# Causal attention core: six bf16 copies of queries and keys against two float32r parts in two row tiles of TensorE

## What is computed

```
q = rope(q); k = rope(k)                      # 32 query heads, 8 key/value heads, head size 16
scores = einsum('bqhd,bkhd->bhqk', q, k) / 16 # 4 query heads share a key head
scores = where(causal, scores, -inf)          # 1024 x 1024 per head
ctx = einsum('bhqk,bkhd->bqhd', softmax(scores), v)
out = ctx @ w_dense.T + b_dense
```

## Time and profile before

| | us |
|---|---|
| median of 3 runs | 1276.73 |
| the profiled execution, own time | 1276.3 |
| its span, first to last instruction | 1274.5 |
| projections block (from its first transposes) | 343 to 403.4 |
| prologue of the core (maxima of group 0) | 403.4 to 438.9 |
| groups 0 to 7 | 438.9 to 687.1 |
| output product | 687.1 to about 720 |

### The profile page before, as it was taken

How to read it: one execution, slowest core, us unless ns; L and a number is a source line. 1 busy time by engine, 2 the same in 40 slices (tenths; PEclk the granted TensorE clock), 3 DMA queues, 4 the chain that set the end, 5 groups by cost and what they waited for, 6 DMA issues and landing times. The chain is left out here.

```text
span 1274.5 us, 21579 instructions
## 1 busy us (share of the span) xinstructions
PE 1097.4 (86%) x5654; PEld 717.9 (56%) x5655; DVE 905.9 (71%) x1775; ACT 704.8 (55%) x1218; POOL 566.7 (44%) x582
## 2 busy tenths in 40 slices
PE   4969999999194899999997787999999947878597
PEld 3847777777182233333333675677777735467454
DVE  5869888887575888888860666888888847444632
ACT  3238787887143177777775131787888824424142
POOL 4335666664556244443331225566666545140200
PEclk9979999999596599999998888999999977989889
DMA  9367899764615550000000183789995561000001
GB/s 351 114 220 185 218 243 286 174 114 60 192 50 155 104 99 19 1 1 1 1 1 1 63 309 111 236 196 258 275 222 103 83 156 67 1 1 1 0 1 66
DMA packets 62798, 151.01 MB, mean 118 GB/s; under 512 B 12224, under 2 KB 17024, under 8 KB 58240
## 3 DMA queue, kind: packets, MB, share of 16 engines
q1 hardware_dynamic: 37440, 95.17, 22.3%
q0 software_dynamic: 22592, 50.27, 20.3%
q10 hardware_dynamic: 2688, 4.65, 1.1%
HBM read 104.89 MB, written 44.97 MB: 118 GB/s over the span
## 5 line engine op out<-in xcount | busy, mean ns | idle before, releaser
L811 POOL DMA_INDIRECT moe_acc_rows<-xn,moe_token_of x94 | 208.0, 2213 | 146.3 <-ACT xn L886 131.1
L923 DVE TENSOR_TENSOR moe_w_lo<-moe_raw,moe_w_hi 128x1536 fp32r<-128x1536 f32 x94 | 165.4, 1759 | 62.9 <-ACT moe_w_hi L874 62.7
L1977 ACT ACTIVATE causal_prob<-causal_sc 128x512 f32<-128x512 f32 (+3 forms) x384 | 166.8, 492 | 70.3 <-PE causal_sc L1882 69.7
L874 ACT CAST moe_w_hi<-moe_raw 128x1536 fp32r x94 | 138.7, 1475 | 78.0 <-issue 76.4
L1864 PE MATMUL causal_mx<-ks,causal_qs 96*128 (+4 forms) x384 | 131.4, 353 | 23.0 <-DMA causal_qs<-causal_parts 16.5
L831 PE MATMUL moe_gu<-moe_w_hi,xt_hi 128*128 128x512 f32 x282 | 148.4, 526 | 0.6 <-DVE moe_w_lo L923 0.6
L1882 PE MATMUL causal_sc<-causal_qs,ks 99*128 (+3 forms) x384 | 120.2, 333 | 1.9 <-ACT causal_prob L1977 1.7
L831 PE MATMUL moe_gu<-moe_w_hi,xt_lo 128*128 128x512 f32 x282 | 111.8, 396 | 0.0
L831 PE MATMUL moe_gu<-moe_w_lo,xt_hi 128*128 128x512 f32 x282 | 110.9, 393 | 0.0
L826 PE MATMUL moe_gu<-moe_raw,xn 128*128 x188 | 98.0, 603 | 5.0 <-ACT moe_w_hi L874 5.0
L1808 POOL TENSOR_SCALAR_AFFINE_SELECT causal_prob<-causal_prob 128x512 f32<-128x512 f32 x64 | 40.9, 639 | 115.9 <-ACT causal_prob L1977 115.5
(11 more groups left out here) (317 smaller groups left out, 2724.5 us busy)
## 6 DMA issues: line engine op xcount, KB each, us to landing
moe_raw<-in_w_gu SPq DMA_DIRECT2D x34, 1024.0 KB, 6.1
moe_raw<-in_w_down SPq DMA_DIRECT2D x34, 512.0 KB, 8.2
causal_qs<-causal_parts SPq DMA_DIRECT2D x45, 128.0 KB, 3.6
moe_acc_rows<-moe_zeros SPq DMA_DIRECT2D x2, 2304.0 KB, 14.7
moe_acc_rows<-x SPq DMA_DIRECT2D x18, 256.0 KB, 2.0
moe_xn_rows<-xn SPq DMA_DIRECT2D x2, 2048.0 KB, 10.7
x<-moe_acc_rows SPq DMA_DIRECT2D x16, 256.0 KB, 6.8
xn<-moe_acc_rows ACTq DMA_DIRECT2D x16, 256.0 KB, 7.2
```

What stands on the lines that cost most here:

```text
L811: pool.indirect_dma_start(acc_rows[a], bass.IndirectOffsetOnAxis(ap=token_of[:, b - 3:b - 2].bitcast(U32), axis=0), out_rows[(b - 3) % OUT ...
L874: nc.scalar.copy(w_hi[1 - s][:, :, :], raw[:, bass.ds(at + SPLIT_AT, GU_COLS - SPLIT_AT)].rearrange("p (k n) -> p k n", k=SPLIT)).then_inc ...
L923: nc.vector.tensor_tensor(w_lo[1 - s][:, :, :], raw[:, bass.ds(at + SPLIT_AT, GU_COLS - SPLIT_AT)].rearrange("p (k n) -> p k n", k=SPLIT), ...
L1977: nc.scalar.activation(prob[u % 2][:, h, o:CH], sc[(u * QPK + h) % BANKS][:, o:CH], ACT.Exp, scale=SCALE).then_inc(exp_done, 1)
```

## The change

Queries and keys are now cut into **two** float32r parts instead of three bf16 ones. Three products of parts suffice, so a stack is 48 rows high. POOL's subtraction writes the second part itself; ACT's second cast and DVE's third part are gone. The maximum has two parts and two rows, so the scores contract over 50 rows.

The stack is held twice. Partitions 0 to 49 serve the scores, partitions 64 to 111 the maxima. A matmul of at most 64 rows is issued to a tile of 64 by 128 of the array: the scores to the tile that starts at row 0, the maxima to the one at row 64. The order of PE's matmuls is unchanged. Both buffers now hold two groups (`g % 2`) in float32, are loaded twice (once per tile), and each load waits until the products that read the old content are done. PE's loop over groups is unrolled, since the addresses are constants.

```diff
-    Q_PART = (0, 0, 1, 0, 1, 2)
-    K_PART = (0, 1, 0, 2, 1, 0)
-    STACK = len(Q_PART) * HD
-    MROWS = 3
+    Q_PART = (0, 0, 1)
+    K_PART = (0, 1, 0)
+    MROWS = 2
+    MAX_AT = 2 * HD
+    SCORE_ROWS = slice(0, 3 * HD + MROWS)
+    MAXIMA_ROWS = slice(64, 64 + 3 * HD)
+    IN_SCORES = (0, HD, 2 * HD + MROWS)
+    IN_MAXIMA = (64, 64 + HD, 64 + 2 * HD)
...
-            nc.gpsimd.tensor_tensor(rest[r % 2][:, :], turned[r % 2][:, :], part[r % NPB][:, 0, :],
-                                    ALU.subtract).then_inc(rest_done, 1)
+            nc.gpsimd.tensor_tensor(part[r % NPB][:, 1, :], turned[r % 2][:, :], part[r % NPB][:, 0, :].bitcast(F32),
+                                    ALU.subtract).then_inc(part_lo_done, 1)
...
-            nc.scalar.copy(part[r % NPB][:, 1, :], rest[r % 2][:, :]).then_inc(p2_done, 1)
...
-            nc.vector.tensor_tensor(part[r % NPB][:, 2, :], rest[r % 2][:, :], part[r % NPB][:, 1, :],
-                                    ALU.subtract).then_inc(p3_done, 1)
...
# SP, the core: loads
-                    with sp.Fori(1, KV) as g:
-                        sp.wait_ge(stack_in, g * (16 * LOADS) - 16 * LOADS // 2)
-                        load(g)
+                    load(IN_MAXIMA, 1, for_maxima_in)
+                    for g in range(KV - 1):
+                        if g:
+                            sp.wait_ge(sc_done, g * NS * QPK)
+                        load(IN_SCORES, g + 1, for_scores_in)
...
+                        if g + 2 < KV:
+                            sp.wait_ge(mx_done, (g + 1) * NMU)
+                            load(IN_MAXIMA, g + 2, for_maxima_in)
...
# PE: maxima
-                        nc.tensor.matmul(mx[i % BANKS][:, 0:w], qs[0:STACK, bass.ds(at, P)],
-                                         ks[0:STACK, bass.ds(gn * S + kc * CH, w)], start=True, stop=True).then_inc(mx_done, 1)
+                        nc.tensor.matmul(mx[i % BANKS][:, 0:w], q_r[MAXIMA_ROWS, at:at + P], k_r[MAXIMA_ROWS, key:key + w],
+                                         start=True, stop=True).then_inc(mx_done, 1)
# PE: scores
-                        nc.tensor.matmul(sc[b][:, o:CH], ks[0:STACK + MROWS, bass.ds(g * S + kb * P, P)],
-                                         qs[0:STACK + MROWS, bass.ds(g * QG + (h * S + c * CH + o), CH - o)],
-                                         start=True, stop=True).then_inc(sc_done, 1)
+                        nc.tensor.matmul(sc[b][:, o:CH], k_r[SCORE_ROWS, key:key + P], q_r[SCORE_ROWS, at + o:at + CH],
+                                         start=True, stop=True).then_inc(sc_done, 1)
...
-                    group(0, True, True)
-                    with pe.Fori(1, KV - 1) as g:
-                        group(g, False, True)
-                    group(KV - 1, False, False)
+                    for g in range(KV):
+                        group(g, g == 0, g < KV - 1)
```

More of the change, by code:

```diff
@@ L1420, in sem, with load_keys @@
             return m.semaphore(f"{name}_{what}")
-        parts_dram = nc.dram_tensor(f"{name}_parts", [3, QK_ROWS, S], BF16, kind="Internal").ap()
-        v_all, ks, ident = m.v_all, m.ks, m.ident_half
-        consts, stack_in, ones_done = sem("consts"), sem("stack_in"), sem("ones_done")
+        parts_dram = nc.dram_tensor(f"{name}_parts", [2, QK_ROWS, S], F32, kind="Internal").ap()
+        v_all = m.v_all
+        ks = outer.enter_context(nc.sbuf_tensor(f"{name}_keys", [P, 2 * 2 * S], BF16))[:, :]
+        for_scores_in, for_maxima_in, ones_done = sem("for_scores_in"), sem("for_maxima_in"), sem("ones_done")
+        def load_keys(eng, rows, g, done):
+            at = g % 2 * S
+            for a, row in enumerate(rows):
+                eng.dma_start(ks.bitcast(F32)[row:row + HD, at:at + S],
+                              parts_dram[K_PART[a], g * HD:(g + 1) * HD, :]).then_inc(done, 16)
         dense_in, wd_half, wd_ready, x_biased = sem("dense_in"), sem("wd_half"), sem("wd_ready"), sem("x_biased")
@@ L1445, in causal_attention_layer @@
             turned = [sb(f"turned{s}", [P, CH]) for s in range(2)]
-            rest = [sb(f"rest{s}", [P, CH]) for s in range(2)]
             NPB = 4
-            part = [sb(f"part{s}", [P, 3, CH], BF16) for s in range(NPB)]
+            part = [sb(f"part{s}", [P, 2, CH], F32R) for s in range(NPB)]
             vt = sb("vt", [P, S])
@@ L1582, in _ @@
                     act.wait_ge(c_in, 48)
-                    for n in range(UNITS + 4):
+                    for n in range(UNITS + 2):
                         if n < UNITS:
@@ L1664, in _ @@
                     lo(T - 1)
-                    for n in range(2, UNITS + 4):
+                    for n in range(2, UNITS + 1):
                         if n in number:
@@ L1700, in causal_attention_layer @@
             neg = sb("neg", [P, TC, QPK])
[L1701 to L1703 removed]
+            neg_parts = [sb(f"neg_parts{h}", [P, TC, MROWS, QPK], F32R) for h in range(NCH)]
+            neg_turned = [sb(f"neg_turned{h}", [MROWS * QPK, CH]) for h in range(NCH)]
             prob = [sb(f"prob{s}", [P, QPK, CH]) for s in range(2)]
@@ L1986, in group @@
                                 read_maxima(g + 1, 0)
-                    for a in range(1, len(Q_PART), 2):
-                        first_queries(act, a)
+                    load_queries(act, IN_MAXIMA, 0, 1, for_maxima_in)
+                    for a in range(len(Q_PART)):
+                        load_queries(act, IN_SCORES, 0, a, for_scores_in)
                     nc.scalar.activation(warm[:, :], m.ident[0:1, 0:1], ACT.Exp).then_inc(exp_done, BANKS)
```

100 lines of the change are left out of this document (41 added, 59 removed).

## The result

The changed kernel takes 1353.42 us (median of 4 runs, 1344.75 to 1360.92) against 1276.55 of before (4 runs as well): ratio 1.0603, interval 1.0532 to 1.0674, slower. The prediction said 1261.5 and faster, and was wrong. The profiled execution took 1344.75 us, its span 1343.0. It was the fastest of the four: the profiles differ by 68.5 us, the medians by 76.9. What follows takes the 68.5 apart.

A forecast was written before the change was run, and what follows sets the result against it. Three nearly equal needs per group (PE 28.7 us, DVE 26.3, the exponential-to-score circle 27.9) were taken as bound, tied by PE's fixed order. Terms of 12.6 + 2.0 + 0 + 0.4 = 15.0 us off gave about 1261.5 us, range 1250 to 1270.

The forecast's parts named there:

- SP's loads stand at nothing: Groups: 12 DMAs, 2 MB, issued at a group's start and needed 29 us later, so priced at no cost.
- rival D: Groups: PE's thinner work lets the clock fall to about 0.5; +60 us, near 1340; chance 0.04.
- Rival B: Groups 1 to 6: loads delay POOL's maxima rows before step 4, up to 1.9 us each; 1272.5 us; chance 0.20.
- Term 3: Core's start: PE's wait for the first queries, 6.5 us into the core, taken as unchanged, 0 us.
- Group 7 held 1.00 with PE busy 22.1 of 27.9 us: Group 7, before the change: full clock without maxima, cited against the falling clock of rival D.
- Term 1: Groups: score and maxima matmuls run side by side in two tiles; groups 1 to 6 take 29.6 us, 12.6 us off altogether.
- C (no overlap): Groups: the two tiles do not overlap, so PE stays the largest need; 1289 us, slower; chance 0.11.
- Rival A: Groups: full relief, DVE and the circle run past each other; groups take 27.4 us, 1246 in all; chance 0.10.
- Term 2: End of the projections: the last unit's shorter way to DRAM takes 2.0 us off, bounds 1.0 and 2.6.
- Term 4: Prologue: DVE-bound, 25.0 us of work, nearly unchanged; 0.4 us off, bounds 0 and 0.8.

The follow-up runs named there:

- late_loads: Changed kernel, but SP issues a group's twelve loads only after its second-half maxima rows have landed: 1312.4 us, in three rounds 1309.0 (ratio 1.0238).
- bf16_pair: Kernel before with 48-row bf16 stacks in both tiles, three of six products left out, loads far ahead, PE's loop unrolled: 1282.9 us.
- full7: late_loads with group 7's scores from step 1 over the whole array, and the mask loaded before the first queries: 1303.4 us.
- bf16_pair7: bf16_pair with group 7's scores from step 1 over 112 rows, the whole array: 1278.9 us, ratio 1.0021.
- whole_f32r: Changed kernel's float32r parts without row tiles: scores and maxima over 66 rows on the whole array, one copy, loads late: 1306.5 us.
- unrolled: Kernel before with PE's loop over groups 1 to 6 written out, nothing else: 1276.4 us, in five rounds 1275.4 (ratio 1.000).
- stack4: Kernel before with four bf16 products instead of six, scores over 67 rows (whole array), maxima in a 64-row tile, PE's loop unrolled: 1462.3 us.

## Why the prediction was wrong

**The two steps that failed** are "SP's loads stand at nothing" and the dismissal of rival D.

- *Loads.* The step asked when the loads themselves are needed, not what stands behind them. Rival B named the place, the instructions and the direction, and was priced at 1.9 us a group from the earlier trace rows, where other loads were under way. The runs show waits of up to 7.9: POOL's rows waited until nearly all of the loads in front were through, which took 16 to 17 us and not rival B's 6 to 11. Even with those numbers the issue after 6.5 us (now up to 9) should have been priced as the rest of the queue. 33 us, and 3 more in the prologue, where the mask and the first queries stood among bytes needed later. Term 3 was right on PE's first matmul (6.3 us into the core for 6.5) and missed DVE's wait for the mask:

```profile
409.93 0.70 DVE L2006 CUSTOM_DVE_ANT_0 causal_mx<-causal_mx,causal_no_later 128x512 f32<-128x512 f32 x1 [18.36 <-DMA causal_no_later<-in_later]
```

- *Clock.* "Group 7 held 1.00 with PE busy 22.1 of 27.9 us" was read as proof that thin work is enough. That row is of the whole array. On a 64-row tile alone the same group falls to 0.5 for most of its time (0.59 in after and late_loads, 0.54 in bf16_pair), on the whole array it has 0.89 to 0.94 (full7, bf16_pair7, whole_f32r). Price: 11.8 us in group 7; 6.5 in group 0, where the clock rose at 463.6 and not at 442.9 (no run takes this apart from its prologue); and 14.5 us of dips in groups 1 to 5 with the loads mended. That D's 1340 lies near the measured 1353 is chance: it gave the clock 60 us for thin work in the groups, the clock took 33, and the loads made up the rest.

**What held.** Term 1's mechanism: pairs start together, 0.24 to 0.28 us apart; C (no overlap) is out. Its size, 29.6 us, is what the bf16 pair shows where the clock is full; with float32r it is 30.9 (after's group 6), so 0.5 us a group is left of 1.8. Float32r itself makes most of the difference: 1.2 us a group between whole_f32r and unrolled. Rival A is out with it.

**Term 2** gave half a us at most: from the layer's first transposes to the last product of the projections it is 52.8 us before and 53.2 after, and the core's first maximum follows 71.5 and 71.0 later. It was put at 2.

**Term 4** is swamped by the wait for the mask; DVE's work is 25.3 us (10.0 + 8.0 + 7.3) for the earlier trace rows's 25.0.

The pieces together: 33.1 (loads) + 14.5 (dips) + 11.8 (group 7) + 6.5 (group 0) + 3.8 (prologue) less 0.4 (group 6) are 69.3. The execution came 3.6 us earlier to the layer, and lost 3.1 behind the groups. Why it lost them stays open; late_loads, with the same change, needs 587.1 us there, as before (587.4). That is the 68.5 within 0.3. What the trace does not give is a rule for when a pair of tiles dips; it was seen at different steps in executions of one and the same kernel.

## What to carry to other kernels

A small DMA that something waits for is priced by all the bytes queued in front of it, not by its neighbours' slowdown: put the bulk behind it, or split it off. A clock observed for one tile shape did not carry over to another here: before 64-row tiles replace whole-array matmuls, look for a stretch where such tiles run alone, and count the tile's gain at both clocks. A gain of 2 us a group is small against a clock that can halve for 10.

## What the runs showed of the hardware

- TensorE can be busy 61.4 of 61.4 us and be granted 1.2 GHz throughout, with 64-row tiles and the whole array in turn (stack4, group 1).
- A change between the 64-row tile and the whole array costs 0.10 us at the full clock (0.32 for 0.22), at every matmul that makes it.
- Loads with 4096-byte packets moved no more per time: the block with them shows 120 GB/s at a DMA share of 0.73, with 2048-byte packets 135 at 0.67. The Trainium skill, "Perfetto Trace Analysis", DMA Optimizations, says that batching small transfers, as from 2 to 4 KB, can improve throughput; here, with loads of 16 partitions, the trace does not agree.
